# Cross-attention and quantised feed-forward on one core: head-pair weights over 128 rows, and four smaller moves

## The reference

```python
x = x + xattn(_layernorm(x), ctx)            # x (8,56,128), ctx (8,1500,96)
#   q = x @ Wq, k = ctx @ Wk, v = ctx @ Wv; softmax(q k^T / 8) v; @ Wout + bout
x = x + ffn(_layernorm(x))
#   xq = fake_quant(x); gate = xq @ q(w_gate).T; up = xq @ q(w_up).T
#   h = fake_quant(silu(gate) * up); h @ q(w_down).T
```

## Time and profile before

| | |
|---|---|
| median of 3 runs | 183.73 us |
| the runs | 179.39, 183.73, 184.19 us |
| profiled execution, its own time | 180.12 us |
| its span | 178.0 us |
| PE / PEld busy | 171.8 / 142.8 us |
| VectorE / ScalarE / GpSimd busy | 145.1 / 133.2 / 127.8 us |
| HBM traffic over the span | 63 GB/s |

### The profile page before, as it was taken

One profiled execution on the slowest core, in us unless ns is written; L12 is line 12 of the kernel. 1 busy time (PEld: TensorE's weight loads), 2 busy tenths in 40 slices (PEclk: granted clock), 3 DMA queues, 4 the chain that ended last, 5 costly groups with the idle time before them and its releaser, 6 DMA issues.

```text
span 178.0 us, 2925 instructions
## 1 busy us (share of the span) xinstructions
PE 171.8 (97%) x876; PEld 142.8 (80%) x877; DVE 145.1 (82%) x345; ACT 133.2 (75%) x284; POOL 127.8 (72%) x135
## 2 busy tenths in 40 slices
PE   7999999999999999999999999999999999999783
PEld 3775878888888889888888898888888888889431
DVE  6596669879975996899988968999989769958785
ACT  3387987868879995778878857788787777865732
POOL 5797599999995887789887856899787775443010
PEclk9999999999999999999999999999999999999999
DMA  5768910270026001900082009000500000000001
GB/s 166 208 171 225 241 36 2 59 204 4 0 85 174 0 0 18 242 3 2 0 220 45 0 0 243 20 0 0 131 0 2 4 0 0 0 0 2 4 0 52
DMA packets 8587, 11.41 MB, mean 64 GB/s; under 512 B 4532, under 2 KB 6772, under 8 KB 8572
## 3 DMA queue, kind: packets, MB, share of 16 engines
q1 hardware_dynamic: 8156, 10.83, 23.8%
q10 hardware_dynamic: 416, 0.40, 0.8%
HBM read 10.97 MB, written 0.23 MB: 63 GB/s over the span
## 4 chain that ended last, share of the span: by engine, by line
PE 86%; DVE 6%; ACT 5%; issue 1%; DVEq 0%; POOL 0%; ACTq 0%; POOLq 0%
PE p_m L1032 11%; PE p_n L1073 11%; PE p_sw L1054 10%; PE p_sw L1046 10%; PE p_n L1081 10%; PE p_n L1075 10%; PE p_sw L1047 10%; PE p_n L979 2%; PE p_n L1089 1%; ACT q_hi L485 1%; ACT e_hi L535 1%; PE p_m L1016 1%; DVE h_flat L937 1%; PE p_n L1016 1%; PE p_sw L994 1%
## 5 line engine op out<-in xcount | busy, mean ns | idle before, releaser
L376 POOL TENSOR_TENSOR e_lo<-e_full,e_hi 125x448 fp32r<-125x448 f32 x48 | 55.8, 1162 | 25.4 <-ACT e_full L538 24.2
L535 ACT ACTIVATE e_hi<-p_sw 125x448 fp32r<-125x448 f32 x96 | 52.2, 544 | 23.4 <-PE p_sw L1054 23.1
L686 DVE TENSOR_REDUCE chunk_max<-p_m 112x1 f32<-112x500 f32 x84 | 55.6, 672 | 15.3 <-PE p_m L1032 14.1
L1046 PE MATMUL p_sw<-q_hi,ctxT_lo 96*125 96x448 f32 x96 | 36.1, 376 | 0.0
L1054 PE MATMUL p_sw<-q_hi,ctxT_hi 97*125 97x448 f32 x96 | 35.5, 370 | 0.0
L1047 PE MATMUL p_sw<-q_lo,ctxT_hi 96*125 96x448 f32 x96 | 35.1, 365 | 0.0
L1073 PE MATMUL p_n<-e_hi,ctx_hi 125*128 125x448 f32 x93 | 34.5, 370 | 0.0
L1081 PE MATMUL p_n<-e_lo,ctx_hi 125*128 125x448 f32 x93 | 33.9, 365 | 0.0
L1075 PE MATMUL p_n<-e_hi,ctx_lo 125*96 125x448 f32 x93 | 33.9, 364 | 0.0
L702 DVE TENSOR_TENSOR e_lo<-p_n,e_hi 125x448 fp32r<-125x448 f32 x48 | 29.6, 616 | 4.5 <-ACT p_n L552 4.3
L1032 PE MATMUL p_m<-ctxT_hi,q_hi 96*112 96x500 f32 x84 | 31.9, 392 | 0.1
(11 more groups left out here) (261 smaller groups left out, 210.4 us busy)
## 6 DMA issues: line engine op xcount, KB each, us to landing
ctx_in<-ctx_d SPq DMA_DIRECT2D x8, 504.0 KB
ctxT_in<-ctxT_d SPq DMA_DIRECT2D x7, 562.5 KB, 6.0
ctxT_in<-ctxT_d SPq DMA_DIRECT2D x3, 187.5 KB, 4.2
q_hi<-maxima SPq DMA_DIRECT2D x30, 0.4 KB, 1.9
ctx_in<-ctx_d SPq DMA_DIRECT2D x8, 58.5 KB
wout<-wout_d SPq DMA_DIRECT2D x1, 256.0 KB, 7.8
...
```

The lines of the kernel that those rows point to most:

```text
L376: pool.tensor_tensor(e_lo[:, k, :], e_full[:, k, :], e_hi[:, k, :], ALU.subtract)\
L535: act.activation(e_hi[:, k, :], p_s[n % 2][0:KT, 0:HQ], ACT.Exp, scale=SCALE)\
L686: dve.reduce_max(chunk_max[:, c // NM, c % NM:c % NM + 1], p_mb[c % NM][0:GQ, 0:MC], AX.X)\
L1046: pe.matmul(o, ctxT_lo[b % 2][:, keys], q_hi[0:C, b, :], start=True, stop=False)
```

## The change

There are five edits.

1. **Weights over 128 rows.** `wqkT` gets 448 columns for each pair. Partitions 0 to 63 hold the even head's key weights, its query weights, and 96 zeros; partitions 64 to 127 hold 96 zeros, the odd head's query weights, and its key weights. The query weights are in the same columns for both. One matmul over 128 rows and two blocks of 96 columns makes both heads' products, in one PSUM bank. The load is split into even and odd halves. For pair 0 the even half is on SyncE's queue and the odd half on ScalarE's, where both halves of pair 1 follow. ScalarE writes the zeros, for pair 0 at the start and for pairs 1 to 3 behind the first copy.
2. **Fillers.** The second group of fillers has 6 matmuls instead of 8.
3. **Rows of maxima.** `row(g)` writes 128 equal rows instead of one; the copy still reads row C.
4. **Keys of the second batch, and query 4.** Two of the three `ctxT_hi` casts of batch 1 move from ScalarE (n = 2 and n = 4 in the loop) to VectorE, behind its maxima of batch 0. `query(4)` moves ahead of the third score matmul of tile 0.
5. **The output's factor.** VectorE's multiply moves ahead of the casts to bf16.

```diff
-        wqkT = sb("wqkT", [2 * DH, HP, D + C])
+        wqkT = sb("wqkT", [2 * DH, HP, 2 * (C + D)])
...
-        qk_banks = [p_s, p_nb[0:2], p_s, p_s]
+        qk_banks = [p_s[0], p_nb[0], p_s[0], p_s[0]]
+        wk_blocks = wqkT.rearrange("p j (k c) -> p j k c", k=2)[:, :, :, 0:C]
...
+        def load_qk_even(eng, pairs, loaded):
+            eng.dma_start(wqkT[0:DH, pairs, 0:C + D], wqk_even_d[:, pairs, :]).then_inc(loaded, 16)
+
+        def load_qk_odd(eng, pairs, loaded):
+            eng.dma_start(wqkT[DH:2 * DH, pairs, C:2 * C + D], wqk_odd_d[:, pairs, :]).then_inc(loaded, 16)
...
-            sp.dma_start(wqkT[:, 0, :], wqkT_d[:, 0, :]).then_inc(qk_loaded[0], 16)
+            load_qk_even(sp, slice(0, 1), qk_loaded[0])
...
-            sp.dma_start(wqkT[:, 2:HP, :], wqkT_d[:, 2:HP, :]).then_inc(qk_loaded[2], 16)
+            load_qk_even(sp, slice(2, HP), qk_loaded[2])
+            load_qk_odd(sp, slice(2, HP), qk_loaded[2])
...
-            act.dma_start(wqkT[:, 1, :], wqkT_d[:, 1, :]).then_inc(qk_loaded[1], 16)
...
+            load_qk_odd(act, slice(0, 1), qk_loaded[0])
+            load_qk_even(act, slice(1, 2), qk_loaded[1])
+            load_qk_odd(act, slice(1, 2), qk_loaded[1])
+
+            def zeros_beside(first, end):
+                for k, at in enumerate((C + D, 0)):
+                    act.activation(wqkT[k * DH:(k + 1) * DH, first:end, at:at + C],
+                                   filler[k * DH:(k + 1) * DH, :].unsqueeze(2).to_broadcast([DH, end - first, C]), ACT.Copy)\
+                        .then_inc(s.zeros_made, 1)
+
+            act.wait_ge(s.filler_made, 1)
+            zeros_beside(0, 1)
...
-            copy_wqk(0, p_sw)
+            copy_wqk(0)
+            zeros_beside(1, HP)
...
-                if n in (2, 4):
-                    ctxT1_hi(n // 2)
...
+            wait_ctxT_in(dve, 1)
+            dve.wait_ge(s.ctxT1_hi_made, 1)
+            for k in range(1, NM):
+                dve.tensor_copy(ctxT_hi[1][0:C, key_piece(k)], ctxT_in[1][:, key_piece(k)]).then_inc(s.ctxT1_hi_made, 1)
...
+            dve.tensor_tensor(hs[:, 0:1], hs[:, 1:2], wscale[:, 6:7], ALU.mult).then_inc(s.y_step, 1)
             dve.wait_ge(s.h_step, 4)
...
-            dve.tensor_tensor(hs[:, 0:1], hs[:, 1:2], wscale[:, 6:7], ALU.mult).then_inc(s.y_step, 1)
...
-                    pe.wait_ge(qk_loaded[j], 16)
+                    pe.wait_ge(qk_loaded[j], 32)
+                if j < 2:
+                    pe.wait_ge(s.zeros_made, 2 * j + 2)
...
-                at = C if j == HP - 1 else 0
-                for k in range(2):
-                    rows = slice(k * DH, (k + 1) * DH)
-                    last = pe.matmul(qk_banks[j][k][:, at:at + C], wqkT[rows, j, 0:D], wqkT[rows, j, D:D + C], start=True, stop=True)
-                return last
+                at = 2 * C if j == HP - 1 else 0
+                return pe.matmul(qk_banks[j][:, at:at + 2 * C], wqkT[:, j, C:C + D], wk_blocks[:, j, :, :], start=True, stop=True)
...
-            busy(8, p_x, 128)
+            busy(6, p_x, 128)
...
-                return pe.matmul(p_mb[2][C:C + 1, g * GQ:(g + 1) * GQ], maxima[0][:, g:g + 1], ident[0:GQ, 0:GQ],
+                return pe.matmul(p_mb[2][:, g * GQ:(g + 1) * GQ], maxima[0][:, g:g + 1].to_broadcast([GQ, 128]), ident[0:GQ, 0:GQ],
...
             scores_lo(0)
+            query(4)
...
-                    for h in LOOP_QUERIES[t]:
+                    for h in LOOP_QUERIES[t][1 if t == 0 else 0:]:
```

29 lines of the change are left out of this document (13 added, 16 removed).

## The result

| | before | after |
|---|---|---|
| median of 22 runs each | 179.88 us | 181.36 us |
| lowest, highest | 178.94, 184.28 | 179.78, 182.54 |
| plain mean | 181.55 us | 181.12 us |
| profiled execution, its own time | 180.12 us | 181.63 us |
| its span | 178.0 us | 179.6 us |

The ratio of after to before is 1.0087, 95% interval [1.0065, 1.0109]: slower by 0.9%, where the forecast was 0.4% faster. That 181.36 us lies inside the predicted range of 178.7 to 184.4 us says little, because the base under it moved by nearly 4 us. All ratios here leave out executions over 1.5% above the fastest of their kernel; for the kernel before these are the ones near 184 us, of which the changed kernel has none, so its plain mean is even 0.4 us lower.

The account below looks back on a forecast made before the run. TensorE, busy for 97% of the span, was taken as the bound. Terms of -0.34 and -0.36 us summed to -0.70, taken off the three-run median of 183.73 us for 183.0 us; range 178.7 to 184.4.

Parts of the forecast that it names:

- pair 0's load: First weights: odd half, second on ScalarE's queue, lands at 4.25 us; value 0, bounds -0.1 and +0.35 us.
- Rival 3: At the first weights PE waits at most 0.35 us and its clock rises much later: 187.5 us; chance 0.06.
- Rival 1: Early stage: full rows and fewer gaps raise PE's clock early in more runs: 179.4 or 178.7 us; chance 0.30.
- Pairs 2 and 3: Merged weight matmuls: chunks end 0.14 us earlier without gaps, 0.24 later with them; value 0, bounds -0.1 and +0.25.
- Rows of maxima and query 4: Tile 0's scores: idle load goes, query 4 precedes the third part; -0.34 us, or -0.17 if the gap stays.
- Casts on VectorE: Second batch's keys: two casts of 0.42 us fit VectorE's idle time, PE's wait near 24 us goes; -0.36 us.
- PE waits for no GpSimd result in it: Steady stretch, 26 to 158 us: PE is busy throughout, so everything ahead moves it as a whole.
- The prediction's mark for this: Sign the forecast is wrong: VectorE's casts of the second batch's keys reach past 16.9 us.
- The tail: Output's factor, a 0.15 us multiply, moves ahead of the casts: 0, bounds -0.1 and +0.1 us; same length.
- The zeros: Four short ScalarE activations, together under 1 us, in a stretch where ScalarE stood idle: cost 0.
- The base: The sum was taken off 183.73 us, the median of three runs shown, not the profiled execution's 180.12.

Follow-up runs that it names:

- e1: Changed kernel with pair 0's odd half issued on SyncE's queue behind its even half, not on ScalarE's; median 179.50 us, ratio to before 1.0016.
- e2: Kernel before with its weight loads split into halves of 64 partitions on the changed kernel's queues, matmuls over 64 rows; median 182.99 us, ratio 1.0027.
- e4: Changed kernel with only the 128-row weights, their loads and zeros, and two fillers fewer; the other parts undone; median 181.03 us, ratio to before 1.0068.
- e14: Changed kernel with GpSimd's low part of query 1 moved from tile 8 to tile 10; median 180.52 us of 6, ratio to before 1.0047.
- e6: e1 with VectorE's two casts of batch 1's keys moved behind the low parts of queries 2 and 3; median 180.65 us, ratio to before 1.0030.
- e7: e1 with eight fillers in the second group instead of six; median 180.20 us, ratio to before 1.0027.
- e12: e1 with the two key casts of batch 1 back on ScalarE at tiles 2 and 4; median 180.81 us, ratio to before 1.0060.
- e9: Changed kernel with pair 0 loaded by one transfer over 128 partitions on SyncE's queue, zeros included; median 179.52 us, ratio to before 1.0013.
- e13: e9 with GpSimd's low part of query 1 moved from tile 8 to tile 10; six runs, 178.55 to 180.74 us, ratio to before 0.9981.
- e17: e13 with VectorE's two key casts behind the low parts of queries 2 and 3, as in e6; median 179.07 us, ratio to before 0.9994.
- e10: Changed kernel with pair 0's odd half issued first on ScalarE's queue, ahead of the tokens; median 181.47 us of 6, ratio to before 1.0104.
- e3: Kernel before with wide maxima rows, query 4 earlier, two casts on VectorE and the output's factor moved; median 179.38 us, ratio 0.9978.
- e5: e1 with each pair's product again as two 64-row matmuls, each into its own bank; median 179.67 us, ratio to before 0.9986.
- e8: Kernel before with only maxima rows 128 wide and query 4 ahead of the third score matmul; median 181.92 us, ratio 1.0013.
- e15: Kernel before with GpSimd's low part of query 1 moved from tile 8 to tile 10; runs 179.58 to 183.69 us, ratio 1.0001.
- e16: Against e1, pairs 0 and 1 stay merged, pairs 2 and 3 take two 64-row matmuls; six runs, 179.38 to 180.60 us, ratio to before 1.0010.
- e11: e1 with only pairs 2 and 3 merged, pairs 0 and 1 over 64 rows; 11 runs, 179.09 to 182.52 us, ratio to before 1.0005.

## Why the prediction was wrong, step by step

**The step that failed: pair 0's load.** The prediction took the landing of the odd half from "what stood there took 2.9 us to land", so 4.25 us, "value 0, bounds -0.1 and +0.35". It landed 4.1 us after its issue, PE waited 1.24 us, and the start moved by 1.43. That the wait comes from this load is shown by e1 (half moved: loss gone), e2 (half without the merged matmul: wait there) and e4 (weights alone: full loss).

What the wait costs has two parts. Like against like it is its length: in the profiled executions of e1 and e14 the clock rose early, their weights start at 4.53 and 4.99 us and their single chunks end at 8.41 and 8.86, and the groups of the changed kernel lie 0.4 and 0.6 us above e1's. The larger part is that PE more often stays at 1.2 GHz longer, at a price of 5.14 - 3.87 = 1.27 us for the same work. Of the runs of kernels with all pairs merged, by how pair 0 is loaded, this many are in the lower group:

| pair 0's load | kernels | first weights start at | lower group |
|---|---|---|---|
| odd half second on ScalarE's queue | after, e4, e14 | 4.99 to 5.46 us | 9 of 39 |
| both halves on SyncE's queue | e1, e6, e7, e12 | 4.53 to 4.80 | 24 of 47 |
| one transfer on SyncE's queue | e9, e13, e17 | 4.17 to 4.54 | 23 of 30 |

(The groups are split at each kernel's widest gap. e10, where PE waits 1.21 us elsewhere, has 2 of 6.) The later the weights, the rarer the early rise. Chance alone would make as large a difference between the first two rows about once in 70 times, and between the first and the third far more rarely. The kernels ran on different chips and differ in more than the load, and no run moved the start alone, so this link is likely and not shown. The Trainium skill, "DMA: Bandwidth & Descriptors", Rules for kernel authors, advises against two transfers to disjoint partition halves and for one over 128 partitions; e9 agrees (160 KB in 2.9 us), and I had not weighed that rule. What makes 4.1 us of it stays open: the pair 1 halves on the same queue took 2.7 and 2.8 us in e1, and 3.7 and 4.4 in e9.

**Rival 3** named this wait and bounded it at 0.35 us. Its second half, that the clock then rises later, came too, though not as far as it said: in the profiled execution between 8.9 us (two records of a chunk still take 1.13) and 9.8, where before it had been about 7. Against the kernel before that is 0.32 us in this pair; against the early rise of e14 it is 1.27, and 18 of 22 runs are of the later kind.

**Rival 1** was right in its mechanism. All kernels with every pair over 64 rows have a group of runs at 182.7 to 184.6: 10 of 22, 10 of 34, 10 of 35, 13 of 29, 6 of 11 and 10 of 19 runs of the kernel before, 8 of 12 in e2, 5 of 12 in e3 and in e5, 5 of 11 in e8, 2 of 5 in e15. All kernels with merged pairs (after, e1, e4, e6, e7, e9, e10, e12 to e14, e17: 122 runs) end by 182.54 us. The later group there is at 180.3 to 182.5. I gave it 0.30 and a time of 179.4; what kept after from it is the wait and the later rise that goes with it. The Trainium skill, "TensorE: Matmul & The Clock Gate", Part 1, says that the point of the rise varies from run to run; the traces now show it. Up to here e3 and the kernel before do the same work, and PE is at 2.4 GHz only past 13 us in one and from about 7 in the other. Likewise e14 and the changed kernel, at 2.4 GHz by 6.32 us in one and only by 9.8 in the other.

**Pairs 2 and 3**: from chunk to chunks 1.49 us before, reckoned as 1.35 without gaps (and put at no change), measured 1.33 in after and 1.32 in e1. The gaps went with the change of form, and the longer stream took most of it, as reckoned. It did not reach the end: from there to the maxima rows' end it is 17.76 - 11.93 = 5.83 us, against 15.93 - 10.34 = 5.59 before; e4, with merged pairs and one-row maxima, has 5.71, so half of the 0.24 is the wider rows.

**Rows of maxima and query 4**: forecast -0.34, measured -0.33: from the rows' end to the third score part of tile 1 it is 18.26 - 15.93 = 2.33 us before and 19.76 - 17.76 = 2.00 after. The wider rows took 0.12 ahead of that, where up to 0.08 was reckoned. The interaction was missed: by itself the gain is given back at tile 5 (e8, e12).

**Casts on VectorE**: forecast -0.36, measured -0.38 at tile 6. But the price of a cast, 0.42 us from VectorE's own first casts with no large GpSimd instruction beside them, was wrong beside GpSimd's `ctx_lo`: 1.74 us for two in after, 2.33 in e1, 0.74 in e6 and e17, where GpSimd is idle for most of them. The prediction's mark for this, casts past 16.9 us, was hit: they end at 18.89, or 17.1 with the 1.8 us of the shift taken off. In e1, e5 and e16 it costs 0.42 to 0.48 us at tile 2, in e14 0.08 and in e9 nothing.

**"PE waits for no GpSimd result in it"** was true of the trace before and false of what follows. I asked what is late next and answered with ScalarE alone. GpSimd, without a pause from its `e_lo` at 22.88 us on, set tile 12 as soon as PE was over 0.41 us quicker than before from there: the piece had ended at 34.18 us, PE starts 0.24 behind it when it waits (36.31 - 36.07), and tile 12 had started at 34.83. That took back 0.42 to 0.48 us in after, e3, e6, e7 and e9 to e11, all about 0.8 us quicker from tile 0 to tile 6, and nothing in e1, e5, e12 and e16, which were 0.36 us quicker at most. e13 to e15 show that it is GpSimd's piece.

**The tail**: from the first step of `h` to the first output it is 176.66 - 174.91 = 1.75 us, against 175.10 - 173.32 = 1.78 before. Nothing, as forecast. The zeros took 0.58 and 0.91 us in after, 1.49 together where under 1 was reckoned, and cost nothing either: they end at 7.77, and the first queries are done at 8.42.

**The base.** I took the sum off 183.73, the median of three. The sum on the profiled execution was 179.4, and that base would have been the better one: of the 22 runs 12 lie by it. By luck the forecast of 183.0 and the measured 181.36 are not further apart: the base was 3.9 us too high and the change 2.2 us too good.

Sum for the profiled execution: +1.43 later start, +0.32 up to the single chunk, +0.08 up to the maxima rows' end, -0.33 query 4, -0.38 casts, +0.43 tile 12, together +1.55, against 179.6 - 178.0 = +1.6 in the span. The version with the wait and both holes taken away has -0.78 on nearly the same clock: the two terms of the forecast, -0.70, were right in size for a kernel that was not the one I was given. In the times of the lower groups that kernel wins 0.4 us.
